# Three phases of windowed attention on one core: the engines' loops are written out straight

## The reference, cut to what matters

```
h = layer_norm(x)                      # over the 48 channels
h = roll(h, (-3, -3)) if shifted       # rows and columns
win = windows of 7 x 7 tokens          # 64 windows an image
q, k, v = split(win @ qkv_w + qkv_b)   # 6 heads of 8
a = softmax(q*8**-0.5 @ k.T + bias (+ mask if shifted))
x = x + unwindow(a @ v) @ proj_w + proj_b
x = x + gelu(layer_norm(x) @ w1 + b1) @ w2 + b2   # 48 -> 192 -> 48
```

## Time and profile before

| | |
|---|---|
| median of 3 runs (lowest to highest) | 5472.18 us (5471.5 to 5475.9) |
| the profiled execution's own time | 5478.46 us |
| its span, first to last instruction | 5476.5 us |
| TensorE matmuls busy | 5300.4 us, 97% |
| VectorE, ScalarE, GpSimd busy | 77%, 73%, 66% |
| mean granted TensorE clock | 0.966 of full speed |

### The profile page before, as it was taken

One profiled execution on the slowest core, in us unless ns is written; L12 is line 12 of the kernel. 1 busy time (PEld: TensorE's weight loads), 2 busy tenths in 40 slices (PEclk: granted clock), 3 DMA queues, 4 the chain that ended last, 5 costly groups with the idle time before them and its releaser, 6 DMA issues.

```text
span 5476.5 us, 249903 instructions
## 1 busy us (share of the span) xinstructions
PE 5300.4 (97%) x102530; PEld 3552.8 (65%) x102530; DVE 4225.1 (77%) x7241; ACT 3998.4 (73%) x6155; POOL 3597.7 (66%) x3737
## 2 busy tenths in 40 slices
PE   6699999999999999999999999999999999999987
PEld 3466666666666666666666666666666666666655
DVE  6678787887888777777777777877887878778864
ACT  0177777777777778777778787877787777777760
POOL 4477766766767666666666666677776677676740
PEclk7599999999999999999999999999999999999995
DMA  7311111111111111111111111111111111111119
GB/s 226 119 31 29 31 29 29 31 29 29 31 29 31 29 29 31 29 31 28 30 29 31 29 29 31 29 30 30 29 32 29 29 31 29 29 31 29 31 53 273
DMA packets 288443, 238.91 MB, mean 44 GB/s; under 512 B 43576, under 2 KB 282906, under 8 KB 287002
## 3 DMA queue, kind: packets, MB, share of 16 engines
q1 hardware_dynamic: 246802, 179.90, 12.4%
q0 software_dynamic: 8192, 22.49, 1.2%
q10 hardware_dynamic: 32282, 20.03, 1.2%
HBM read 112.93 MB, written 109.36 MB: 41 GB/s over the span
## 4 chain that ended last, share of the span: by engine, by line
PE 93%; DMA 4%; issue 1%; DVE 1%; SPq 0%; POOL 0%; ACT 0%; DVEq 0%; ACTq 0%; POOLq 0%
PE pB L1091 10%; PE pA L1103 10%; PE pB L1079 10%; PE pS L1067 10%; PE pS L1113 6%; PE pA L1079 6%; PE pS L1040 5%; PE pA L1134 5%; PE pS L1155 5%; PE pS L1079 4%; PE pA L1055 4%; PE pS L1165 3%; PE pS L1145 3%; PE pB L1017 3%; PE pA L1017 3%; PE pB L1009 2%
## 5 line engine op out<-in xcount | busy, mean ns | idle before, releaser
L463 POOL TENSOR_TENSOR S<-S,mx 113x588 f32<-113x588 f32 x1536 | 1786.1, 1185 | 21.9 <-DVE mx L810 21.9
L797 DVE TENSOR_TENSOR S<-pS,bias 113x588 f32<-113x588 f32 x1536 | 1113.0, 767 | 819.7 <-PE pS L1067 819.7
L449 POOL TENSOR_TENSOR Kbd<-KT,headmask 128x588 f32<-128x588 f32 x768 | 896.1, 1167 | 1094.4 <-DVE KT L819 1094.4
L810 DVE TENSOR_REDUCE mx<-S 113x12 f32<-113x588 f32 x1536 | 1126.4, 754 | 0.1
L493 POOL TENSOR_TENSOR xn<-x,rs 112x392 f32<-112x392 f32 x384 | 390.9, 1018 | 450.6 <-ACT rs L566 450.5
L555 ACT ACTIVATE sq<-pB 112x392 f32<-112x392 f32 x384 | 190.9, 497 | 657.6 <-PE pB L1009 657.6
L1079 PE MATMUL pB<-ident,S 113*113 113x113 f32 x4608 | 620.5, 271 | 0.3
L838 DVE COPY V<-pA 49x192 f32<-49x192 f32 x1536 | 545.5, 355 | 72.0 <-PE pA L1055 4.8
L1091 PE MATMUL pB<-E,V 113*32 113x98 f32 x18432 | 597.6, 248 | 0.8 <-issue 0.8
L1067 PEld LDWEIGHTS pS<-Kbd,Qt 24*49 24x49 f32 x24576 | 355.6, 117 | 368.9 <-issue 368.9
L1103 PE MATMUL pA<-E,keyones 113*32 113x392 f32 x4608 | 593.1, 503 | 1.8 <-ACT va L559 1.7
(11 more groups left out here) (134 smaller groups left out, 8875.3 us busy)
## 6 DMA issues: line engine op xcount, KB each, us to landing
xin<-xT SPq DMA_DIRECT2D x384, 98.0 KB, 2.0
xT<-xout SPq DMA_DIRECT2D x384, 98.0 KB, 1.9
xin<-xT SPq DMA_DIRECT2D x384, 73.5 KB, 2.0
xT<-xout SPq DMA_DIRECT2D x384, 73.5 KB, 1.8
xT<-cm POOLq DMA_DIRECT2D x128, 171.5 KB, 3.8
cm<-xT SPq DMA_DIRECT2D x128, 171.5 KB, 3.4
tm<-in_x SPq DMA_DIRECT2D x128, 147.0 KB
out<-tm ACTq DMA_DIRECT2D x128, 147.0 KB
```

Source lines behind the costliest of these rows:

```text
L449: return pool.tensor_tensor(y, x, m, ALU.mult)
L463: pool.tensor_tensor(s, s, m, ALU.subtract).then_inc(sub_done[half][wh], 1)
L797: dve.tensor_tensor(strided(S[:, b, w, 0, 0, 0:1], [[KEYS, 2], [2 * KEYS, 2 * HP], [1, N]]), strided(pS[0:M2, 2 * wh, 0:1], [[512, 2], [N, ...
L810: dve.tensor_reduce(m, s, AX.X, ALU.max).then_inc(mx_done[half][wh], 1)
```

## The change

`sweep` loses its loops. All 389 iterations (384 steps and the five that drain the pipeline) are written out one after the other on each engine, with the step number a constant. Order, tiles, buffers and the values waited for stay as they were. What the register served (the values of waits, SyncE's addresses) becomes constant, and the bodies of 40 iterations, read three times each before, become 120 iterations that are each read once. The loops of the transposition back stay.

```diff
         def sweep(eng, iteration):
 
             ahead = (0, -1, -2, -3, -4, -5, -6)
-            begin = 7
-            full = (STEPS - begin - 1) // UM
-
-            def peeled(i):
+            for i in range(NPH * STEPS + LAST):
                 iteration(*(Step(0, (i + k) % STEPS, (i + k) // STEPS, UM) if 0 <= i + k < NPH * STEPS else None
                             for k in ahead))
-
-            for i in range(begin):
-                peeled(i)
-            for t in range(NPH):
-                with eng.Fori(0, full) as u:
-                    for k in range(UM):
-                        iteration(*(Step(u, begin + k + o, t, UM) for o in ahead))
-                for i in range(begin + UM * full, STEPS + (begin if t < NPH - 1 else LAST)):
-                    peeled(i + t * STEPS)
-
```

## The result

The straight kernel takes 5431.19 us (median of six runs, 5428.95 to 5433.05) against 5474.32 us for the kernel before (median of six runs, 5471.5 to 5480.52). The ratio is 0.992, with a 95% interval of 0.9907 to 0.9932: 43.1 us less, where 43.5 us were forecast. The profiled execution took 5432.85 us, its span is 5431.1 us.

The account below looks back on a forecast made before the run. TensorE, busy 97% of the span, was taken to bound the kernel. From the runs' median of 5472.2 us, 43.5 us for six jumps came off, other terms counting nothing: 5428.7 us, range 5416 to 5445 us.

Parts of the forecast that it names:

- The price of the jumps: Six jumps back in the three step loops, priced by step cadence: 43.5 us gained, 7.2 us each.
- GpSimd's late restart: After its loop branch GpSimd resumes 2.8 us later, read as delaying the second long step; not priced separately.
- Register work: Loops' register additions, taken as hidden, gain nothing; the rival had them exposed, 11.5 us more gain, 5417 us, chance 0.07.
- New instructions instead of the same ones: TensorE's instruction queue reading straight code once instead of loop bodies repeatedly: no extra cost.
- The slower rival: Unrepeated instructions fetched late, 0.1 us for each of TensorE's 840 packets: 40.5 us slower, 5513 us, chance 0.04.
- Small stalls, 13.09 us a step: Undisturbed steps keep their short issue waits and 13.09 us average in straight code, with 6 us allowed either way.
- Rival 1: All steps run at the straight stretches' 13.22 us: 5476 us, chance 0.03; half the effect, 5452 us, 0.03.
- Rival 2: Each loop jump costs only its short branch and the stalls stay: 5471.5 us, chance 0.03.
- Rival 3: Only TensorE's named wait ahead of an iteration's first work goes, 18.1 us: 5454 us, chance 0.04.

## Why the prediction was right

**The price of the jumps.** Right as a sum: 43.5 us by the cadence, 7.2 us a jump, against 45.4 us (7.6 us a jump) by taking the jumps alone away and 95.5 us for twelve. Pricing by the cadence of the steps was what made it right, since it took in the second wait and the low clock without my having to know them. That 43.1 us came out for 43.5 is luck, though: the faster small steps (9.5 us), the later first addition (6 us), the longer end (1.6 us) and the scatter between executions happened to cancel.

**How it splits.** Wrong in its attribution. "GpSimd's late restart" as the cause of the second long step was read from one jump of six. TensorE's own jumps are 39.1 us of it, with a second wait at two of them and up to 17 us of low clock. The late restarts of the others overlap with it, and when they stand alone VectorE, ScalarE and SyncE cost more than GpSimd (9.8 against 5.5 us), ScalarE's at the first two jumps above all. In the prediction this was reading, not a term of the sum, so it cost nothing there; it would have, had only one engine's loops gone.

**Register work, nothing.** Right: with registers and without jumps, 5432.5 us.

**New instructions instead of the same ones, nothing.** Right: 833 packets against 846, steps no longer. The slower rival falls.

**Small stalls, 13.09 us a step.** The one mis-sized term. They came out at 13.07 us, 9.5 us less, more than the 6 us allowed; over the six traces without a costly jump (4924.3 to 4929.3 us for the 377 steps) it is 6 to 11 us less. Rival 1 falls: the same two stretches of 8 steps, 105.6 and 105.9 us before, take 104.0 and 104.3 us in the straight kernel. They were two places where the stream of instructions, by my reading, met its bad places more often: 8 iterations hold only some 17 multiples of 256. A mean over 16 steps of something that recurs every 27 was no sample.

**The rivals by price.** Rival 2 would have left 5471.5 us. The trace bears a short branch out wherever it falls through (67 to 85 ns on TensorE) or the body is short (53 ns on GpSimd), and the time refutes it as the price of these jumps. The Trainium skill's page "Advanced Engine Details and Errata", section "Control Flow Timing", gives about 108 ns for a compare-and-branch; no branch measured here fits it, neither the short ones of 34 to 85 ns nor TensorE's jumps, 0.2 us in the transposition back and 3.8 to 4.3 us in the long loops. Rival 3, 5454 us, falls with the clock: without the jumps it has no drop between 279 and 5260 us.

## What to carry to other kernels

Price a hardware loop's jump by the cadence of the work around it, not by the branch's duration: here 7.6 us a jump, of which the named wait was 3 us. Before writing a loop out, count the instructions of its body on each engine. Four engines with bodies of 8 iterations jumped 42 times for nothing, and the long body on the engine that bounds the kernel cost 0.7% with six jumps. Read every instance of a stall before putting it down to an engine; the first one lacked the wait that made the longest.

## What the runs showed of the hardware that I had not expected

A jump back on TensorE can wait twice: 2.51 us ahead of the first work and 1.63 us after 13 matmuls. The DMA record of the kernel before shows how. At its third jump the branch ends at 2512.65 us, the next packet of instructions leaves only at 2513.31 us and lands at 2514.22 us, and TensorE goes on 1.41 us later. At the first jump the packet behind the branch comes just as late (824.50 to 825.52 us after a branch that ends at 823.84 us), but TensorE doesn't run dry. The likely reason is how many instructions the first packet holds behind the jump's target; no run moved the target.

Each standstill of TensorE ahead of `down_c` at its jumps, 2.3 to 4.3 us, was followed by 3.4 to 17 us at the lower clock, and no other stretch between 279 and 5260 us of the straight kernel had one. It isn't the jump that lowers it: a wait of 2.0 us for ScalarE, with TensorE straight, was followed by 3.4 us at 1.2 GHz too. One of 2.1 us in the run with four engines looped was not. Semaphore increments on TensorE's queue that nobody waits for start 160 ns apart while showing 51 ns each. And a straight stream of instructions has small stalls of its own, 0.2 to 1.2 us, at places that recur with 256 instructions.
